# Splat attention preparation: logit jobs in pairs inside and behind the projections, turned maxima in another bank, one weight split over two engines

## What is computed

```
qkv = (x @ qkv_w.T).reshape(b, t, 3, h, hd)
q, k, v = (qkv[:, :, 0], qkv[:, :, 1], qkv[:, :, 2])
def splat_weights(tok):
    d2 = sum(tok ** 2, -1)[..., None] + c_sq - 2.0 * einsum('bthd,hsd->bths', tok, centers)
    return exp(-d2 * inv_var) * eff_amps
qw = splat_weights(q)
kw = splat_weights(k)
logits = einsum('bihs,bjhs->bijh', qw, kw) / temp
attn = softmax(logits, axis=2)
out = einsum('bijh,bjhd->bihd', attn, v).reshape(b, t, d)
return out @ out_w.T
```

## Time and profile before

| what | value |
|---|---|
| median of 3 runs | 872.32 us (871.96 to 872.9) |
| the profiled execution, whole | 871.7 us |
| its span, first to last instruction | 869.9 us |
| busy in the span: PE, DVE, ACT, POOL | 780.6, 618.6, 382.3, 115.9 us |
| mean granted TensorE clock | 0.951 of full |
| the stage: first p to first E | 531.6 to 670.7 us of the span |

### The profile page before, as it was taken

How to read it: one execution, slowest core, us unless ns; L and a number is a source line. 1 busy time by engine, 2 the same in 40 slices (tenths; PEclk the granted TensorE clock), 3 DMA queues, 4 the chain that set the end, 5 groups by cost and what they waited for, 6 DMA issues and landing times. The chain is left out here.

```text
span 869.9 us, 11646 instructions
## 1 busy us (share of the span) xinstructions
PE 780.6 (90%) x4057; PEld 576.1 (66%) x4058; DVE 618.6 (71%) x1224; ACT 382.3 (44%) x583; POOL 115.9 (13%) x90
## 2 busy tenths in 40 slices
PE   4989999998999970995899999898788999999998
PEld 3777878887878750663587778655455566665776
DVE  7767887776849657698844223488786788898656
ACT  2352343332313312565111114756522788887453
POOL 3000000000000005012280002432700012000000
PEclk9999999999999995898599999999998899999999
DMA  5572322210302235996321102000000000010002
GB/s 181 153 232 82 104 69 74 74 38 8 122 3 94 80 142 157 310 377 221 86 95 44 55 0 98 1 1 2 2 1 3 2 1 1 1 55 2 1 1 97
DMA packets 48152, 66.63 MB, mean 77 GB/s; under 512 B 4268, under 2 KB 22460, under 8 KB 48095
## 3 DMA queue, kind: packets, MB, share of 16 engines
q1 hardware_dynamic: 43903, 56.22, 19.8%
q0 software_dynamic: 2384, 6.92, 2.5%
q10 hardware_dynamic: 1808, 2.75, 0.9%
HBM read 56.38 MB, written 9.50 MB: 76 GB/s over the span
## 5 line engine op out<-in xcount | busy, mean ns | idle before, releaser
L952 PE MATMUL bank<-xT,slot 128*128 128x512 f32 (+1 forms) x248 | 106.5, 429 | 2.7 <-DVE xT L1753 2.3
L953 PE MATMUL bank<-xT,slot 128*128 128x512 f32 (+1 forms) x248 | 98.7, 398 | 0.0
L954 PE MATMUL bank<-xT,slot 128*128 128x512 f32 (+1 forms) x248 | 98.4, 397 | 0.0
L1456 ACT ACTIVATE slot<-bank 128x512 fp32r<-128x512 f32 (+3 forms) x60 | 34.1, 586 | 137.9 <-PE bank L1216 56.3
L952 PE MATMUL bank<-slot 128*128 128x512 f32 (+1 forms) x212 | 83.8, 395 | 4.0 <-issue 1.8
L2282 DVE TENSOR_REDUCE key<-bank 128x2 f32<-128x1024 f32 x64 | 75.1, 1217 | 14.3 <-PE bank L1276 14.3
L954 PE MATMUL bank<-slot 128*128 128x512 f32 (+1 forms) x212 | 81.5, 384 | 0.0
L953 PE MATMUL bank<-slot 128*128 128x512 f32 (+1 forms) x212 | 81.2, 383 | 0.0
L952 PE MATMUL bank<-slot,xT 128*128 128x512 f32 (+1 forms) x192 | 79.0, 411 | 0.9 <-DVE xT L2134 0.9
L1681 ACT ACTIVATE arena<-bank 128x1024 f32<-128x1024 f32 x64 | 65.6, 1027 | 26.8 <-PE bank L1344 25.0
L954 PE MATMUL bank<-slot,xT 128*128 128x512 f32 (+1 forms) x192 | 76.6, 399 | 0.0
(11 more groups left out here) (336 smaller groups left out, 1638.5 us busy)
## 6 DMA issues: line engine op xcount, KB each, us to landing
arena<-in_ewT SPq DMA_DIRECT2D x16, 1024.0 KB, 11.4
arena<-in_edge_attr SPq DMA_DIRECT2D x16, 512.0 KB, 4.0
wraw<-in_qkvT SPq DMA_DIRECT2D x3, 1024.0 KB, 5.1
expert_rows<-rows SPq DMA_DIRECT2D x1, 2560.0 KB, 13.8
wraw<-in_L_ffn_expert_b POOLq DMA_DIRECT2D x16, 160.0 KB, 5.7
expert_results<-wraw ACTq DMA_DIRECT2D x16, 160.0 KB, 5.7
xn<-in_x SPq DMA_DIRECT2D x4, 512.0 KB, 6.5
wraw<-in_L_mix_w_qkv SPq DMA_DIRECT2D x2, 1024.0 KB, 8.0
```

Source lines behind the costliest of these rows:

```text
L952: pe.matmul(out, L[1], R[0], start=start, stop=False, **kw)
L953: pe.matmul(out, L[0], R[0], start=False, stop=False, **kw)
L954: return pe.matmul(out, L[0], R[1], start=False, stop=stop, **kw)
L1456: act.activation(h, src, kw.pop("func", ACT.Copy), **kw).then_inc(hi_done, 1)
```

## The change

1. **The order of logit jobs.** A new table `logits_about(job)` says how many logit jobs stand inside a job, in the middle of its 12 matmuls (behind the second of the four chunks), and how many behind it. For a projection it is two inside and two behind, except for the first of a block (q, th = 0): none inside, two behind. For d2 only the second (q, th = 1) has two behind it; the others have none. For the values V1 0 to 7 it is (0, 2), (2, 2), (2, 2), (2, 0), (2, 0), (2, 0), none, none. The count for each head pair stays 16.
2. **Turned maxima.** mT of the stage goes to bank 4 in place of 0. In the block of the values it stands behind V1 5 in place of V1 3.
3. **The split of Lv.** DVE subtracts the first half only, in two instructions of 128 by 512 (`value_weight_low`): one at the old place, one behind the weights of `("d2", "q", 3, 0)`. POOL subtracts the second half, 128 by 1024, behind its 16 subtractions for the squares. V1 0 waits for DVE's half before its first matmul and for POOL's (`values_half`) at its third chunk.

```diff
@@ plan_jobs
-            add(*step, bank=0)
+            add(*step, bank=4)
@@ splat_steps
-            behind = [2] * len(work)
...
-            behind = [2] * T
-        for i, (job, count) in enumerate(zip(work, behind)):
-            steps.append(job)
-            steps += logits[:count]
-            logits = logits[count:]
-            if i == 3 and c > 1:
+        for i, job in enumerate(work):
+            inner, behind = logits_about(job)
+            if c == 0:
+                inner = behind = 0
+            steps += logits[:inner] + [job] + logits[inner:inner + behind]
+            logits = logits[inner + behind:]
+            if i == (3 if c < PAIRS else 5) and c > 1:
                 steps.append(("mT", c - 2))
+def logits_about(job):
+
+    if job[0] == "V1":
+        return ((0, 2), (2, 2), (2, 2), (2, 0), (2, 0), (2, 0), (0, 0), (0, 0))[job[1]]
+    if job[0] == "p":
+        return (0, 2) if job[1] == "q" and job[3] == 0 else (2, 2)
+    return (0, 2) if job[1] == "q" and job[3] == 1 else (0, 0)
@@ gpsimd
+            pool.wait_ge(w_hi, windex["Lv"] + 1)
+            second = slot[0][:, :, TWO:C, :].rearrange("p v c d -> p v (c d)")
+            pool.tensor_tensor(second[:, 1], staging[stage_of["Lv"]][:, TWO * D:C * D], f32(second[:, 0]), ALU.subtract).then_inc(values_half, 1)
+            pool.wait_ge(values_half, 1)
@@ tensor
-            def product(name, L, R, ks=C, waits=None):
+            def product(name, L, R, ks=C, waits=None, between=()):
...
                     ins = mm3(o, L(k), R(k), k == 0, k == ks - 1)
+                    if k == 1:
+                        for other in between:
+                            logits(other)
...
-                    product(step, lambda k: xt(step[1], k), lambda k: sl(0, k))
+                    product(step, lambda k: xt(step[1], k), lambda k: sl(0, k), between=inside[step],
+                            waits=lambda k: step[1] == 0 and k == TWO and pe.wait_ge(values_half, 1))
@@ vector
+            def value_weight_low(k):
+
+                dve.wait_ge(w_hi, windex["Lv"] + 1)
+                raw = staging[stage_of["Lv"]][:, k * D:(k + 1) * D]
+                ins = dve.tensor_tensor(slot[0][:, 1, k, :], raw, f32(slot[0][:, 0, k, :]), ALU.subtract)
+                if k == TWO - 1:
+                    ins.then_inc(w_split, 1)
...
                 if step == ("p", "k", PAIRS - 1, 1):
-                    split_weight("Lv")
+                    value_weight_low(0)
                 elif step[0] == "d2":
                     weights(step)
+                    if step == ("d2", "q", PAIRS - 1, 0):
+                        value_weight_low(1)
```

More of the change, by code:

```diff
@@ L242, in splat_steps, with logits_inside @@
             work += [("d2", side, c, th) for side in "qk" for th in range(2)]
-            behind = [2] * len(work)
         else:
             work = [("V1", t) for t in range(T)]
-            behind = [2] * T
-        for i, (job, count) in enumerate(zip(work, behind)):
-            steps.append(job)
-            steps += logits[:count]
-            logits = logits[count:]
-            if i == 3 and c > 1:
+        for i, job in enumerate(work):
[5 more added lines that the diff above has]
+            if i == (3 if c < PAIRS else 5) and c > 1:
                 steps.append(("mT", c - 2))
+        assert not logits
     return steps
+def logits_about(job):
[4 more added lines that the diff above has]
+    return (0, 2) if job[1] == "q" and job[3] == 1 else (0, 0)
+def logits_inside():
+    steps = splat_steps()
+    return {job: steps[i - logits_about(job)[0]:i] if job[0] == "V1" or job[2] else [] for i, job in enumerate(steps)
+            if job[0] in ("p", "V1")}
 def vector_order():
@@ L582, in build @@
         wh_ready = sem("weights_hi")
+        values_half = sem("values_second_half_low")
         mx_ready = sem("mx_ready")
@@ L1284, in turn_maxima @@
                 close(pe.transpose(o[0:2 * T, 0:P], mx[:, c % 2].rearrange("p b t -> p (b t)"), ident))
+            inside = logits_inside()
+            interleaved = {step for steps in inside.values() for step in steps}
             for step in splat_steps():
@@ L1291, in _ @@
                         pe.wait_ge(w_split, windex[("Lq", "Lk")[n]] + 1)
-                    product(step, lambda k: sl(n, k, c * P, c * P + P), lambda k: hl(xT[th], k))
+                    product(step, lambda k: sl(n, k, c * P, c * P + P), lambda k: hl(xT[th], k), between=inside[step])
                 elif step[0] == "d2":
@@ L1301, in _ @@
                 elif step[0] == "L":
-                    logits(step)
+                    if step not in interleaved:
+                        logits(step)
                 elif step[0] == "mT":
@@ L2270, in maxima @@
                 link(dve.tensor_scalar(mneg[0], o, -1.0, None, ALU.mult))
-                dve.scalar_tensor_tensor(mneg[1], o, -1.0, f32(mneg[0]), ALU.mult, ALU.subtract).then_inc(evicted[0], 1)
+                dve.scalar_tensor_tensor(mneg[1], o, -1.0, f32(mneg[0]), ALU.mult, ALU.subtract).then_inc(evicted[bank_of[step]], 1)
             for step in vector_order():
                 if step == ("p", "k", PAIRS - 1, 1):
-                    split_weight("Lv")
+                    value_weight_low(0)
                 elif step[0] == "d2":
                     weights(step)
+                    if step == ("d2", "q", PAIRS - 1, 0):
+                        value_weight_low(1)
                 elif step[0] == "L":
@@ L2292, in _ @@
                     if step[1] == 0:
+                        dve.wait_ge(st_ready, 4 * PAIRS)
                         dve.memset(f32(vone)[:, 0, :, :, HD:HD + 1], 1.0)
```

## The result

The changed kernel takes 863.01 us as the median of four runs (859.79 to 864.34), the kernel before 872.37: a ratio of 0.9884, 95% interval 0.9862 to 0.9907. In a second measurement, of experiment e5, it was 863.33 and 0.9879 (0.9864 to 0.9894). The forecast was 863.0.

A forecast was written before the change was run, and what follows sets the result against it. PE, busy 780.6 of 869.9 us, bounds the kernel; time is won only where it idles or runs at the lower clock. Terms 0.9 + 2.1 + 4.1 + 3.2 + 0.5 - 1.6 = 9.2 us gave 863.0, range 860.5 to 865.5.

The forecast's parts named there:

- Rhythm of a projection with four jobs: Projections with four logit jobs: 4.9 us each, bounds 4.5 and 5.3, with PE waiting at every second pair.
- A middle block: Blocks 1 and 2: 24.9 us against 25.30 and 26.96, gains 0.9 and 2.1; block 1 keeps a 0.5 shorter first wait.
- mT in bank 4: Turned maxima in the stage: wait nothing, cost 0.13; waits of 1.18, 4.08 and 1.97 us go.
- Lv: End of block 3: first value starts 2.2 us late behind DVE's queue and POOL; block 27.1 us, gain 4.1.
- The hold by POOL: Before the first value: POOL's half of Lv stops DVE's weights until 25.5; wait 2.2 us, against 1.1 side by side.
- Values: Block of the values: 32.9 us against 36.1, gain 3.2; inner waits 0.4 and 0.7; first E finds its bank free.
- Start of the attention: First E to first O: 0.5 us off today's 5.36; the half-clock stretch behind it stays.
- Clock: Behind the 2.2 us wait before the first value: PE falls to 1.2 GHz, 1.6 us lost.
- Ahead of the stage: Before block 1: the prediction's sum has no term for it, so no difference was assumed.
- everything overlaps better: Rival: clock stays up in V1 0, DVE gets ahead of POOL, projections take 4.7; 858.5 us, chance 0.17.
- The middle blocks win nothing: Rival: projections of 5.3 us, blocks 1 and 2 keep their length, block 3 loses 1.2; 867.3 us, chance 0.18.
- The slower one, in which short waits pull the clock down: Rival: PE runs one block at 1.2 GHz, 13.6 us more, giving 876.7; three give 904; chance 0.05.

The follow-up runs named there:

- e5: The changed kernel measured once more, nothing altered: 863.33 us.
- e4: The changed kernel with each logit-job reduction over half of its columns (128x512 in place of 128x1024): 852.48 us, ratio 0.9774.
- e2: The kernel before with only the bank of mT changed, 4 in place of 0, at its old place: 873.86 us, ratio 1.0015.
- e3: The kernel before with only the split of Lv changed (two quarters on DVE, one half on POOL): 869.82 us, ratio 0.9963.
- e12: The kernel before with mT in bank 4 and, among the values, behind V1 5 in place of V1 3: 867.84 us, ratio 0.9930.
- e1: The changed kernel with mT back in bank 0 and the split of Lv back on DVE as one instruction: 863.59 us, ratio 0.9892.
- e9: The changed kernel with mT back in bank 0, all else as changed: 862.33 us, ratio 0.9885.
- e11: The changed kernel with POOL's half of Lv given to DVE as two more pieces behind the second: 858.70 us, ratio 0.9833.
- e10: The changed kernel with the split of Lv back on DVE as one instruction at its old place: 860.76 us, ratio 0.9858.
- e6: The changed kernel with DVE's second piece of Lv directly behind the first: 859.12 us, ratio 0.9839.
- e7: The changed kernel with another values table, four logit jobs in one value only: 858.39 us, ratio 0.9834.

## Why the prediction was right

The time was right to 0.1 us, and most of its steps stand one by one; that the sum is so close is partly luck, as the last points show.

- **Rhythm of a projection with four jobs: right.** 4.9 forecast, 4.97 measured, in all blocks, with the loss at every second pair as forecast. e4 shows the reason given: with DVE's part halved it is PE's 4.5.
- **A middle block: right in size, 24.9 forecast and 24.88 to 24.91 measured.** That block 1 comes out 0.5 shorter was luck. In the first profile, with the lower clock in block 0 (0.92 over it, as in the kernel before), block 1 was 24.28; in e5, with block 0 at full clock, 24.91. What the short first wait of block 1 hangs on is the clock of the block ahead of it: with PE slower there, the weights are ready in time. The gain of 0.9 holds either way: with block 0 at full clock, block 1 is 25.87 or 25.88 in the old order (e2, e3, e12). The first wait of the middle blocks was forecast as 0.8 to 0.9 and is 0.64 to 0.69 beside the usual 0.1 for going over. (Three projections of 4.9 are 14.7, not 14.8; with 14.7 the terms give the 24.9.)
- **mT in bank 4: right for this order.** It waits nowhere. That "the next user of bank 4 is the next projection", far enough off, held. e2 shows how much hangs on this step: where the next user comes sooner, the bank costs more than it gives. And e1 and e9 show that among the values it is the place, and not the bank, that ends the wait.
- **Lv: right in mechanism and size.** 27.1 forecast for block 3, 26.92 measured. The queue on DVE was named in its order. The wait of 2.2 is 0.3 more than the prediction's own terms give: weights and piece behind 25.5 make 26.8, a wait of 1.9, which is what was measured (1.88). The hold by POOL, 1.1 in the forecast and 0.8 in these terms, was measured as 0.8 (e11). It struck another instruction than forecast, the maximum over 16 columns, which stands ahead of the weights and reads two SBUF operands as well; the prediction had left that one out, and the weights took 0.74, as elsewhere. The Trainium skill, page SBUF — State Buffer, section "SBUF: two separate sides", says that the one that starts first keeps the shared ports for its whole instruction and the other fully blocks. The trace agrees, 0.94 against 0.18. What the prediction missed is that the new order removes the collision of the old split by itself, 2.28 in place of 4.33 (e10): the 4.1 is no gain of sharing the split, without which block 3 is shorter still, 26.04.
- **Values: right.** 32.9 forecast (its terms add up to 32.8); 33.04, 32.88, 32.99, 32.96 and 33.11 in five profiles without a fall of the clock, and 33.54 in e6, where a wait had moved into the block. The inner waits of 0.4 and 0.7 are 0.29 and 0.63 beside the 0.1 for going over.
- **Start of the attention: right.** 4.86 forecast, 4.75 measured.
- **Clock: right on the whole, by two errors in opposite directions.** The fall behind the first value's wait was counted whole, 1.6. It is in e5's profile (1.5) and not in the first; the wait was 1.88 both times. The fall behind the start of the attention was left as it was; it is absent in the first profile and about two thirds of its size in e5.
- **Ahead of the stage** the forecast assumed no difference. In the profiles there is one, 0 to 2.8 us. Nothing shows that the change has to do with it: block 1 starts at 552.47 and 553.94 in the same kernel, and between 551.06 and 553.57 in the old order.

Of the rivals, the one in which everything overlaps better (858.5) comes near the first profile's 859.8, but only one of its three conditions held there: the clock stayed up in V1 0, while the hold by POOL came and the projections took 4.97. "The middle blocks win nothing" is excluded by block 2. The slower one, in which short waits pull the clock down, is excluded: blocks 1 to 3 have the clock at 1.00, with a wait of 0.2 in every 5 us, and the values with waits of 0.29 and 0.63 in every 5.8 us too. The Trainium skill, page TensorE: Matmul & The Clock Gate, section "A second HAM failure mode: psum-queue depth-cycling", describes a kernel in which frequent short idles between groups of matmuls made the clock swing. No run here shows that at this size of idling.

What the prediction did not ask is which part gives the gain. The four kernels in the new order answer that; the last column adds the windows of block 2, block 3 and the values.

| in the new order | ratio to the kernel before | windows, us |
|---|---|---|
| order alone (e1) | 0.9892 (0.9877 to 0.9907) | 88.4, clock 0.94 in block 3 |
| with bank 4 (e10) | 0.9858 (0.9840 to 0.9876) | 84.1 |
| with the shared split (e9) | 0.9885 (0.9862 to 0.9909) | 86.8 |
| with both, the change | 0.9884 and 0.9879 | 84.9; 86.3 with the fall of the clock (e5) |

The order brings by far the most, 9.4 of 872.8 us. With the split left whole, the bank brings another 3.0, by intervals that just do not meet, since mT then no longer waits 1.16 and 2.93 and the clock in block 3 is 1.00 in place of 0.94. The shared split brings nothing measurable in time, and with the bank it probably takes some 2 us back. So the fastest of the four is probably not the changed kernel but e10.

## What to carry to other kernels

Walk through the program order of the waiting engine and the engine it waits for, with start-to-start times from the trace, and let each job wait for what frees its bank: here that gave the blocks to 0.2 us, where busy shares say only that both engines have room. When a small job is moved to another bank or queue, look at the next user of that place and at what stands ahead of the reader on its engine. And measure each part again in the new order: the shared split won 3 us before, because a collision made the whole one take 4.33; once the order had changed, the whole one took 2.28 and sharing it won nothing.

## What the runs showed of the hardware

- A DVE instruction over 16 columns took 0.94 us beside a POOL instruction, and 0.18 without it. A 512-column one took 2.73 in place of 0.68 (e3), and one of 2048 columns 4.33 in the kernel before and 2.28 in e10, where it fell between two POOL instructions. The reductions of 128 by 1024 from PSUM were not held: the last two took 2.36 beside POOL's half of Lv, as elsewhere. It was not expected that so small an instruction could be held for so long.
- After a wait of the same length, 1.88 us, the same program had the clock at 1.00 in one execution and at 1.2 GHz for part of the next 6 us in another; after 1.90 it was at 1.00 in e4 and at 0.71 in e7. In block 0 PE waits 2.14 for ACT in every one of the 14 profiles, and the clock falls behind it in two of them (before, and the first of the changed kernel). In e3 it stayed up after 1.98, before the change it fell after 1.97. After waits of 1.08 to 1.31 (e9, e11) it was at 1.00.
- Behind the same instructions, block 1 starts between 551.06 and 553.94 us in the 14 profiles, 1.5 us apart in two of the same kernel, so that the stage's own windows tell two kernels apart better than the total does.
